# Job clusters of two attention segments put together, in a cross-attention and feed-forward kernel on one Trainium2 core

## The reference

```python
# x: (1, 2048, 256); context: (1, 1601, 256); 16 heads of 64
x = x + tanh(g_xattn) * xattn(layernorm(x), context)
#   xattn: lat = LN(latents), ctx = LN(context)
#   q = lat @ Wq ; k, v = split(ctx @ Wkv)
#   attn = softmax(clip(q k^T / 8, -11, 11)) ; out = (attn @ v) @ Wo + bo
x = x + tanh(g_ffn) * ffn(layernorm(x))
#   ffn: gated, inner size 768, with 4-bit weights and 16-bit activations
#   quantised and dequantised by block or by tensor maximum
```

## Time and profile before

| | |
|---|---|
| median of three runs | 1198.07 us |
| the profiled execution, its own time | 1199.25 us |
| its span, first to last instruction | 1197.5 us |
| TensorE busy | 1095.0 us, 91% |
| VectorE busy | 975.2 us, 81% |
| ScalarE busy | 618.3 us, 52% |
| GpSimd busy | 36.8 us, 3% |
| mean granted TensorE clock | 0.965 of full |
| TensorE's share of the chain that ended last | 76% |

### The profile page before, as it was taken

How to read it: one execution, slowest core, us unless ns; L and a number is a source line. 1 busy time by engine, 2 the same in 40 slices (tenths; PEclk the granted TensorE clock), 3 DMA queues, 4 the chain that set the end, 5 groups by cost and what they waited for, 6 DMA issues and landing times.

```text
span 1197.5 us, 20388 instructions
## 1 busy us (share of the span) xinstructions
PE 1095.0 (91%) x8427; PEld 498.3 (42%) x8427; DVE 975.2 (81%) x1320; ACT 618.3 (52%) x714; POOL 36.8 (3%) x45
## 2 busy tenths in 40 slices
PE   3999999999999999999999999999999987897038
PEld 2443344434443444344434443444333322676038
DVE  7467978797879788988898889887888889649976
ACT  2455555555555555555555555555555553459532
POOL 1200000000000000000000000000000000003400
PEclk9999999999999999999999999999999999799559
DMA  5000300010001000100010001000000000000002
GB/s 165 1 1 2 115 1 19 1 36 2 19 1 37 1 19 2 36 1 19 1 36 2 19 1 37 2 19 2 19 10 11 10 10 9 1 1 0 0 1 71
DMA packets 27307, 22.23 MB, mean 19 GB/s; under 512 B 8461, under 2 KB 22990, under 8 KB 27214
## 3 DMA queue, kind: packets, MB, share of 16 engines
q1 hardware_dynamic: 27214, 20.92, 5.8%
HBM read 18.55 MB, written 2.22 MB: 17 GB/s over the span
## 4 chain that ended last, share of the span: by engine, by line
PE 76%; DVE 12%; ACT 5%; issue 4%; POOL 1%; DMA 1%; SPq 0%; POOLq 0%; DVEq 0%
PE ps L1077 26%; PE ps L1061 25%; PE ps L1174 6%; PE ps L971 4%; DVE acc L739 4%; PE ps L979 4%; PE ps L1020 4%; PE ps L988 4%; DVE e_buf L783 3%; PE ps L999 2%; ACT e_buf L503 1%; ACT z L571 1%; ACT z L573 1%; PE ps L960 1%; DVE gt L907 1%
## 5 line engine op out<-in xcount | busy, mean ns | idle before, releaser
L503 ACT ACTIVATE e_buf<-ps 128x1024 f32<-128x1024 f32 x416 | 426.1, 1025 | 312.1 <-PE ps L1061 312.1
L1077 PE MATMUL ps<-e_buf,vb 64*64 64x512 f32 x3328 | 436.1, 594 | 4.0 <-DVE e_buf L783 3.8
L739 DVE TENSOR_TENSOR acc<-acc,e_buf 128x1024 f32<-128x1024 f32 (+1 forms) x352 | 427.1, 1213 | 0.0
L783 DVE TENSOR_SCALAR e_buf<-e_buf 128x1024 f32<-128x1024 f32 x416 | 283.1, 681 | 107.8 <-ACT e_buf L503 107.6
L1077 PEld LDWEIGHTS ps<-e_buf,vb 64*64 64x64 f32 x3328 | 119.9, 133 | 243.4 <-issue 212.2
L1061 PE MATMUL ps<-qb,kb_even 64*64 64x512 f32 x1664 | 215.9, 589 | 1.3 <-ACT e_buf L503 1.3
L1061 PE MATMUL ps<-qb,kb_odd 64*64 64x512 f32 x1664 | 216.0, 589 | 0.0
L1061 PEld LDWEIGHTS ps<-qb,kb_odd 64*64 64x64 f32 x1664 | 63.9, 133 | 115.1 <-issue 115.1
L1061 PEld LDWEIGHTS ps<-qb,kb_even 64*64 64x64 f32 x1664 | 63.6, 133 | 115.2 <-issue 113.6
L775 DVE TENSOR_TENSOR xacc<-ps,xacc 128x512 f32<-128x512 f32 x60 | 40.9, 688 | 51.8 <-PE ps L1020 51.8
L1174 PE MATMUL ps<-hT,wgu 128*128 128x512 f32 x288 | 70.1, 406 | 2.2 <-DVE hT L877 2.2
(11 more groups left out here) (117 smaller groups left out, 631.5 us busy)
## 6 DMA issues: line engine op xcount, KB each, us to landing
rden<-inv_rows SPq DMA_DIRECT2D x62, 128.0 KB, 2.9
xacc<-in_x_dram SPq DMA_DIRECT2D x4, 512.0 KB, 7.6
wst<-in_L_xattn_Wkv_dram SPq DMA_DIRECT2D x16, 128.0 KB, 2.6
out_dram<-z SPq DMA_DIRECT2D x8, 256.0 KB, 2.1
e_buf<-in_ctx_dram SPq DMA_DIRECT2D x3, 512.0 KB, 4.6
wst<-in_L_xattn_Wq_dram SPq DMA_DIRECT2D x8, 128.0 KB, 2.7
wo_raw<-in_L_xattn_Wo_dram SPq DMA_DIRECT2D x8, 128.0 KB, 3.4
den_spread<-den_row SPq DMA_DIRECT2D x62, 2.0 KB, 1.7
```

Source lines behind the costliest of these rows:

```text
L503: nc.scalar.activation(e_buf[:, g % E_BUFS, :, :], sc[:, g % 2, :, :], ACT.Exp, scale=float(DH) ** -0.5).then_inc(exp_done, 1)
L739: dve.tensor_tensor(acc[0:r, t0 % 3, :, :], a, e_buf[0:r, (ST * t0 + st) % E_BUFS, :, :], ALU.add).then_inc(summed, 1)
L783: dve.tensor_scalar(tile, tile, EXP_LO, EXP_HI, ALU.max, ALU.min).then_inc(clip_done, 1)
L1077: ins = pe.matmul(ps_o[DH * h:DH * h + DH, half, :], vb[rows, p % 2, st, DH * h:DH * h + DH], e_buf[rows, g % E_BUFS, h, :], start=(st == ...
```

## The change

Segments 2 to 22 with even t get the jobs of two segments in one cluster: two blocks of k and v, q for t + 1 and t + 2, y for t - 4 and t - 3, then den. The odd segments 3 to 21 have no jobs; segment 23 keeps one y. `qb` gets a third slot and `oT` a fourth. A function `adds_through` says how many sums VectorE has done by each tile: in odd segments 3 to 21 one sum is passed over at tile 6 and one at tile 10, so that from tile 10 two are held back; they are caught up in the next even segment (two sums at tile 0, one at tile 1, before `join_out`, then as before). The while loop replaces the old case distinction; at tile 1 of a segment, where the join is, it gives the same place for the join as before.

```diff
+TWICE0, TWICE1 = 2, SEGS - 2 * NBS - 2
+ADDS = ST - 1
+
+def twice(t):
+    return TWICE0 <= t <= TWICE1 and t % 2 == 0
+
 def kv_blocks(t):
+    if twice(t):
+        return [(t // NBS + 1, t % NBS), (t // NBS + 1, t % NBS + 1)]
+    if t == TWICE1 + 1 or t > 0 and twice(t - 1):
+        return []
     if t < SEGS - 2 * NBS:
-        return [(t // NBS + 1, t % NBS)] if t else [(1, 0)]
+        return [(t // NBS + 1, t % NBS)]
...
+def q_segments(t):
+    if twice(t):
+        return [t + 1, t + 2]
+    if twice(t - 1) or t + 1 >= SEGS:
+        return []
+    return [t + 1]
+
+def adds_through(t, st):
+    done = ADDS * t + (st - 1 if st else 0) if st >= 2 else ADDS * t
+    held = 0
+    if twice(t - 1) and t < TWICE1:
+        held = (st >= 6) + (st >= 10)
+    elif twice(t) and t > TWICE0 and st == 0:
+        held = 1
+    return done - held
+
 def y_segments(t):
+    if twice(t):
+        return [t - 4, t - 3] if t >= 4 else []
+    if t < TWICE1:
+        return []
+    if t == TWICE1 + 1:
+        return [t - 3]
     if t <= WT0:
         return [t - 3] if t >= 3 else []
...
-    if t + 1 < SEGS:
-        jobs += [(0, ("q", t + 1))]
+    jobs += [(0, ("q", s)) for s in q_segments(t)]
...
-            qb = sb("qb", [P, 2, NB], stack=att)
+            qb = sb("qb", [P, 3, NB], stack=att)
...
-            oT = sb("oT", [P, 3, NB], stack=att)
+            oT = sb("oT", [P, 4, NB], stack=att)
...
             def half_out(seg, t):
                 act.wait_ge(pv_done, Seg(t).count(ST, ST))
-                if t >= 3:
-                    await_job(act, ("y", t - 3, 1), seg)
-                nc.scalar.copy(oT[:, t % 3, :], ps_o[:, 0, :]).then_inc(o_half, 1)
+                if t >= 4:
+                    await_job(act, ("y", t - 4, 1), seg)
+                nc.scalar.copy(oT[:, t % 4, :], ps_o[:, 0, :]).then_inc(o_half, 1)
...
                     norm_piece(t0, st, 0)
-                    if st >= 2:
-                        add_e(seg, st - 1)
-                    elif st == 0 and t0 >= 1:
-                        add_e(Seg(t0 - 1), ST - 1)
-                    elif t0 >= 1:
+                    while added[0] < adds_through(t0, st):
+                        add_e(Seg(added[0] // ADDS), added[0] % ADDS + 1)
+                        added[0] += 1
+                    if st == 1 and t0 >= 1:
                         join_out(seg, t0 - 1)
```

More of the change, by code:

```diff
@@ L436, in q_take @@
                 await_job(act, key, seg)
-                nc.scalar.copy(qb[:, t % 2, :], ps_m[:, bank_of(key), :]).then_inc(job_taken[bank_of(key)], 1)
+                nc.scalar.copy(qb[:, t % 3, :], ps_m[:, bank_of(key), :]).then_inc(job_taken[bank_of(key)], 1)
             def k_take(seg, p, b):
@@ L520, in run @@
                             v_take(seg, p, b)
-                        if t0 + 1 < SEGS:
-                            q_take(seg, t0 + 1)
+                        for t in q_segments(t0):
+                            q_take(seg, t)
                         if turn_in(t0) is not None:
@@ L664, in h_tops @@
                     z[:, 4 * b:4 * b + 4, :].rearrange("p (a t) d -> p a (t d)", a=2)).then_inc(h_top, 1)
+            added = [0]
             def norm_piece(t0, st, place):
@@ L759, in scale_out @@
                 dve.wait_ge(o_out, Seg(t).count(1, 1))
-                dve.tensor_tensor(oT[:, t % 3, :], oT[:, t % 3, :], rden[:, DENS[i].index(t), :], ALU.mult).then_inc(norm_done, 1)
+                dve.tensor_tensor(oT[:, t % 4, :], oT[:, t % 4, :], rden[:, DENS[i].index(t), :], ALU.mult).then_inc(norm_done, 1)
             def join_out(seg, t):
@@ L765, in join_out @@
                 dve.wait_ge(o_half, s.count(1, 1))
-                dve.tensor_tensor(oT[:, t % 3, :], ps_o[:, 1, :], oT[:, t % 3, :], ALU.add).then_inc(o_out, 1)
+                dve.tensor_tensor(oT[:, t % 4, :], ps_o[:, 1, :], oT[:, t % 4, :], ALU.add).then_inc(o_out, 1)
             def add_y(seg, t, half):
@@ L830, in _ @@
                     await_taken(dve, ("den", t))
-                dve.tensor_tensor(oT[:, t % 3, part], oT[:, t % 3, part], rden[:, 0, part], ALU.mult).then_inc(last_norm, 1)
+                dve.tensor_tensor(oT[:, t % 4, part], oT[:, t % 4, part], rden[:, 0, part], ALU.mult).then_inc(last_norm, 1)
             n, at = NT - NBS, LN3 + NT - NBS
@@ L1019, in y_job @@
                     n0 = P * (2 * half + m)
-                    ins = pe.matmul(bank[:, DM * m:DM * m + DM], oT[:, t % 3, n0:n0 + P], wo_g[:, p % 2, :], start=True, stop=True)
+                    ins = pe.matmul(bank[:, DM * m:DM * m + DM], oT[:, t % 4, n0:n0 + P], wo_g[:, p % 2, :], start=True, stop=True)
                 ins.then_inc(job_ready[bank_of(key)], 1)
@@ L1031, in y_last @@
                     n0 = P * (2 * half + m)
-                    ins = pe.matmul(ps_s[:, half, DM * m:DM * m + DM], oT[:, t % 3, n0:n0 + P], wo_g[:, ORDER[t][0] % 2, :],
+                    ins = pe.matmul(ps_s[:, half, DM * m:DM * m + DM], oT[:, t % 4, n0:n0 + P], wo_g[:, ORDER[t][0] % 2, :],
                                     start=(t < SEGS - 1 and m == 0), stop=(t == SEGS - 1 and m == 1))
@@ L1061, in scores @@
                         ins = pe.matmul(sc[at:at + DH, g % 2, h, :], kb[p % 2][rows, P * st + at:P * st + at + DH],
-                                        qb[rows, t0 % 2, :], start=True, stop=True)
+                                        qb[rows, t0 % 3, :], start=True, stop=True)
                 ins.then_inc(scores_ready, 1)
@@ L1134, in run @@
                         elif kind == "q":
-                            q_job(seg, t0 + 1, loaded(ORDER[t0 + 1][0], seg))
+                            q_job(seg, key[1], loaded(ORDER[key[1]][0], seg))
                         elif kind == "k":
```

## The result

The changed kernel takes 1229.24 us (median of four runs, 1228.34 to 1230.84) against 1198.7 before: slower by 30.5 us, ratio 1.025 (95% interval 1.0227 to 1.0274). I had forecast slower, 1218.6, and a range of 1211 to 1228. The sign is right and so is the mechanism that the sum was made of; but a second one, which I had left out of it, makes the rise a third larger, and the range was missed by 1.2 us.

A forecast was written before the change was run, and what follows sets the result against it. TensorE was taken to set the pace in attention; 5 x (2.29 - 0.29) + 5 x (2.36 - 0.29) + 0.17 = +20.5 us gave 1218.6 us, range 1211 to 1228 (own range 1214 to 1222).

The forecast's parts named there:

- What is removed and added on TensorE: Odd clusters of 7.41 or 5.20 us go, jobs of 7.12 or 4.91 join the even cluster before: 0.29 us saved each.
- The wait that takes the cluster's place: At ten odd boundaries values tile 0 waits for the previous segment's join: 2.29 us at five, 2.36 at five.
- Held sums without effect: VectorE sums passed over in odd segments and caught up under the next even cluster cost and gain nothing.
- The sum, +20.5: Segments 2 to 23: ten waits less 0.29 us saved each, 10.0 + 10.35, plus 0.17 at t = 23.
- the clock, made a rival of chance 0.10: Behind the odd-boundary waits the clock halves for 3.4 us, costing 1.7 each; all ten: +17, 1235.6 us; chance 0.10.
- half the boundaries, 1227: Half-speed stretches of 3.4 us follow the new waits at half of the ten odd boundaries: 1227 us.
- The rule on rotating PSUM banks: Independent matmul groups should rotate PSUM banks; by it only the emptying is exposed at odd boundaries, +9.2 us, 1207.3; chance 0.06.
- The third rival, not slower,: At odd boundaries the join is done when scores tile 2 ends, so only switches are saved: 1195.2 us; chance 0.06.

The follow-up runs named there:

- sums held ahead of the boundary: Changed kernel with the two held-back sums passed over at tile 11 of the even segment and tile 0 of the odd one: 1204.38 us.
- two fill matmuls: Changed kernel with two 128x512 matmuls of no use between scores tile 2 and values tile 0 at odd t from 3 to 21: 1219.65 us.
- longer waits, empty: Changed kernel with two VectorE scalings by 1.0 ahead of the join at the ten odd boundaries: 1256.27 us.
- longer waits, filled: Changed kernel with two VectorE scalings ahead of the join at ten odd boundaries and three 128x512 matmuls of no use under each wait: 1236.6 us.
- the execution with four falls: Changed kernel, no edit, profiled a third time; four stretches at half clock, segments 1 to 23 take 706.8 us.
- two further edits: Changed kernel with two sums held back before the odd boundary and scores tile 3 issued before values tile 0 at odd t: 1197.3 us.

## Why the prediction was right and wrong, by its own steps

- **What is removed and added on TensorE, 0.29 saved for each pair: right.** The double clusters are 13.29 and 15.46 us long against 13.24 and 15.45 by my terms, so a pair saves 0.24 or 0.28.
- **The wait that takes the cluster's place, 2.29 and 2.36: right**, with the rows' lateness carried over unchanged. From start to start it is 2.24 and 2.30, with 0.05 for the tile behind it. That VectorE is what is late is shown by the sums held ahead of the boundary, which cut 2.3 to 0.9 us. That the two products of scale_out are what makes it late is read from the rows alone (1.10 where none stands before the join); no run moved them.
- **Held sums without effect: right**, shown by undoing them.
- **The sum, +20.5: right for what it counted.** With TensorE kept from idling the same waits cost 20.9. The half clock below comes on top.
- **What failed is the step behind it: the clock, made a rival of chance 0.10 instead of a term.** I argued that each wait stands between tens of microseconds of dense matmuls. The traces say that a wait of 2.3 us is enough by itself, though not every time: 2, 3 and 4 of ten in three executions of this kernel, 1.7 us each, 3.4 to 6.8 us. I had the price right, 1.7, and even a case near the truth (half the boundaries, 1227), but centred the range on none. The dense work around a wait did not keep the clock up. Filling the wait gives back 9.6 us at the median.
- **Is the clock enough for the whole of the missing 10 us?** In the traces the falls explain 3.4 to 6.8. For all runs there are the span and the mean granted clock, and twice (1 - clock) times the span is the time at half clock in the whole program, good to about 1.2 us for one run. Half of it is what it costs if all of it costs what it does in dense work; the last column is the span without that.

| kernel (runs) | span, mean | at half clock, mean | span less half of that |
|---|---|---|---|
| before (35) | 1197.4 | 79.2 | 1157.8 |
| changed (4) | 1227.6 | 99.4 | 1177.8 |
| two fill matmuls (4) | 1217.9 | 79.8 | 1178.1 |
| longer waits, empty (4) | 1253.8 | 126.6 | 1190.5 |
| longer waits, filled (4) | 1234.7 | 85.2 | 1192.1 |

By this the change costs 20.0 us in waits less saved switches, where the sum had 20.5, and 10.1 in clock, where it had nothing. The changed and the filled kernel differ in the clock alone. The profiled run of the changed kernel was its best, with 96 us at half clock; the three others had 101, as the execution with four falls.
- **Open:** where those 20 us at half clock lie in the runs of which no trace is shown; in the three traces of the changed kernel 6.8 to 13.7 us lie in segments 1 to 23. The part of the span outside segments 1 to 23 varies from 516.5 to 521.7 us over the thirteen traces. It goes with the time at half clock in that part, 76 to 92 us (correlation 0.84), and stretches come and go there in kernels that the edits leave alike. Why the clock falls behind one wait and not behind the next equal one no run here shows.
- **The rule on rotating PSUM banks** (the Trainium skill, Perfetto Trace Analysis, Optimizing Tensor Performance, Matmuls): the traces agree with it as far as they go. All segments accumulate in one pair of banks, and in the kernel with sums held ahead nearly the emptying alone is exposed, 0.9 us for each boundary. No run here gave the segments a second pair.
- **The third rival, not slower,** needed the join within 0.18 us of the scores. It took two further edits to get there, and then it was worth 3 us of stretch.

## What to carry to other kernels

Before a block of independent work is moved away, list what its time was covering on the other engines: here it was the emptying of the one accumulator pair, late by 2.2 us, against a saving of 0.3. Read that lateness from the trace of before (end of the evacuating instruction minus end of the last work that could go without it) and multiply. When new waits of TensorE like these, 2.3 us in dense work, come out of the sum, count the half clock behind them as a term with a count of its own (here 2 to 4 falls of ten in the traces; none in one trace each with waits of 1.4 and 0.9 us); and where work is held back to relieve an engine, hold it back ahead of the point where someone waits for that engine.

## What was not expected of the hardware

A wait of TensorE of 2.3 us in dense work is followed by 3.4 us at half clock in some executions and at some of ten like places, and not in others: 2, 3, 4 and 4 times in four traces. With 3.7 us of waiting it was eight of ten, some for 6.8 us. Matmuls of no use in the wait, 1.9 of 2.3 us or 2.8 of 3.7, kept the clock at 1.00 in segments 1 to 23 of one trace each, and made the kernel 9.6 and 19.7 us faster.
